# Routed experts of the last feed-forward: token rows sorted by expert on the chip, in place of every expert over every token

## The reference, cut to what matters

```
def _L1_ffn_ref(x, w12, w3, router_w, expert_bias, sw1, sw2, sw3):
    shared_out = jax.nn.silu(x @ sw1.T) * (x @ sw2.T) @ sw3.T
    scores = jax.nn.sigmoid(x @ router_w.T)
    _, top_idx = jax.lax.top_k(scores + expert_bias, 2)
    top_scores = jnp.take_along_axis(scores, top_idx, axis=-1)
    top_scores = top_scores / (top_scores.sum(-1, keepdims=True) + 1e-09)
    ...
    h12 = jnp.einsum('td,ehd->teh', flat_x, w12)
    h1, h2 = jnp.split(h12, 2, axis=-1)
    out_e = jnp.einsum('teh,edh->ted', jax.nn.silu(h1) * h2, w3)
    routed_out = jnp.einsum('ted,te->td', out_e, combine)
    return shared_out + routed_out
x = _layernorm(x + _L1_ffn_ref(x, ...))
```

## Time and profile before

| | us |
|---|---|
| median of 3 runs (lowest, highest) | 1739.21 (1738.74, 1739.77) |
| profiled execution, its own time | 1737.75 |
| its span | 1735.9 |
| last feed-forward, from its first product to its last, each sequence | 144 |

### The profile page before, as it was taken

How to read it: one execution, slowest core, us unless ns; L and a number is a source line. 1 busy time by engine, 2 the same in 40 slices (tenths; PEclk the granted TensorE clock), 3 DMA queues, 4 the chain that set the end, 5 groups by cost and what they waited for, 6 DMA issues and landing times.

```text
span 1735.9 us, 33253 instructions
## 1 busy us (share of the span) xinstructions
PE 1629.3 (94%) x10924; PEld 1401.3 (81%) x10924; DVE 1140.3 (66%) x2654; ACT 936.1 (54%) x1942; POOL 581.2 (33%) x518
## 2 busy tenths in 40 slices
PE   4999999999898999899989999999989989998998
PEld 3888989889787677588878889898988867767887
DVE  7666767676535778455776676766756467765567
ACT  3666565555444577543356655556554437773443
POOL 2554444454460102111126355444555320030120
PEclk9999999999899899999999999999999989999999
DMA  4100000000110423101010000000002123311110
GB/s 132 37 25 16 25 1 15 24 16 1 46 57 15 74 44 67 51 28 46 10 51 23 19 16 25 15 24 0 16 1 64 39 53 56 50 48 43 37 46 25
DMA packets 35213, 60.16 MB, mean 35 GB/s; under 512 B 7989, under 2 KB 22069, under 8 KB 33769
## 3 DMA queue, kind: packets, MB, share of 16 engines
q1 hardware_dynamic: 35064, 58.28, 12.7%
HBM read 42.24 MB, written 3.42 MB: 26 GB/s over the span
## 4 chain that ended last, share of the span: by engine, by line
PE 68%; DVE 11%; ACT 8%; issue 7%; POOL 2%; SPq 1%; DMA 1%; ACTq 0%; DVEq 0%; POOLq 0%
PE ps L346 17%; PE ps L348 16%; PE ps L347 16%; PE ps L901 5%; PE ps L931 4%; PE ps L954 4%; ACT E L1141 3%; DVE nmax L1452 3%; PE ps L762 2%; POOL E L1777 1%; ACT PT_h L1123 1%; DVE On L1394 1%; PE ps L916 1%; PE ps L938 1%; PE ps L701 1%
## 5 line engine op out<-in xcount | busy, mean ns | idle before, releaser
L1141 ACT ACTIVATE E<-ps,nmax 128x128 f32<-128x128 f32 (+7 forms) x256 | 188.8, 741 | 206.9 <-DVE nmax L1452 206.2
L1774 POOL TENSOR_SCALAR E<-E,mixc 128x128 f32<-128x128 f32 (+7 forms) x128 | 97.3, 761 | 381.7 <-DVE mixc L1422 381.7
L1248 ACT ACTIVATE PT<-ps 128x512 f32<-128x512 f32 x288 | 157.9, 599 | 63.4 <-PE ps L938 30.0
L1452 DVE TENSOR_REDUCE nmax<-ps 128x1 f32<-128x128 f32 (+7 forms) x256 | 182.9, 749 | 12.9 <-PE ps L739 12.8
L1777 POOL TENSOR_TENSOR E<-E 128x128 f32<-128x128 f32 (+7 forms) x128 | 182.4, 1425 | 10.7
L1760 POOL TENSOR_TENSOR Fw_l<-Fw_raw,Fw_h 128x768 fp32r<-128x768 f32 x48 | 88.8, 1850 | 262.6 <-ACT Fw_h L1188 261.8
L346 PE MATMUL ps<-V_h,PT_h 128*128 128x256 f32 x576 | 167.5, 291 | 0.0
L346 PE MATMUL ps<-XT_h,Fw_h 128*128 128x512 f32 x384 | 156.4, 407 | 9.0 <-DVE XT_l L1325 9.0
L347 PE MATMUL ps<-V_l,PT_h 128*128 128x256 f32 x576 | 163.1, 283 | 0.0
L348 PE MATMUL ps<-V_h,PT_l 128*128 128x256 f32 x576 | 163.0, 283 | 0.0
L1495 DVE TENSOR_TENSOR Hf<-ps,silu_g 128x512 f32<-128x512 f32 x96 | 66.4, 691 | 140.1 <-PE ps L348 138.0
(11 more groups left out here) (211 smaller groups left out, 4641.4 us busy)
## 6 DMA issues: line engine op xcount, KB each, us to landing
Fw_raw<-in_fa SPq DMA_DIRECT2D x48, 256.0 KB, 2.6
Wa_raw<-in_wa SPq DMA_DIRECT2D x9, 1024.0 KB, 4.9
Wo_raw<-in_wo SPq DMA_DIRECT2D x8, 512.0 KB, 3.9
Fw_raw<-in_fb SPq DMA_DIRECT2D x32, 128.0 KB, 2.6
KS<-QK_h SPq DMA_DIRECT2D x56, 64.0 KB
QS<-QK_h SPq DMA_DIRECT2D x56, 64.0 KB
Xn<-in_x SPq DMA_DIRECT2D x3, 1024.0 KB, 5.8
Fw_raw<-w2s SPq DMA_DIRECT2D x16, 128.0 KB, 2.6
```

Of the source, the lines that this page charges most:

```text
L1141: nc.scalar.activation(e[:, 0:w], ps[m][:, 0:w], ACT.Exp, bias=nmax[:, s % 4, m:m + 1], accum_out=lsum[:, s % 4, m:m + 1]).then_inc(exp_do ...
L1248: nc.scalar.activation(PT[:, at:at + HALF], bank1(RING1 + n % RING1), ACT.Exp, scale=SCALE1).then_inc(t_used, 1)
L1452: nc.vector.tensor_reduce(nmax[:, s % 4, m:m + 1], ps[m][:, 0:(s % NT + 1) * P], AX.X, ALU.max, negate=True).then_inc(nmax_ready[m], 1)
L1774: nc.gpsimd.tensor_scalar(e2, e2, mixc[:, n % 4:n % 4 + 1], 1.0, ALU.mult, ALU.mult).then_inc(mix_scaled, 1)
```

## The change

The 16 expert steps are gone. In their place:

- **Ranks.** The router's portions stand at shared steps 3 to 6, and go on: a product of the picks with a triangle of ones and nine small products on PE (`rank_tokens`) count each token's place among its expert's tokens. DVE adds each expert's first tile and writes the row number as an integer (`place_i`), two per token, and the expert of each of 23 tiles (`expert`). 35 DVE instructions instead of 20.
- **Scatter.** POOL issues 16 indirect DMAs, each sending 128 rows of X (1 KB a row) to their places in `xs` in DRAM, after two of its last three weight splits; the third stands behind the fourth scatter. `xs` is filled first with input rows by three DRAM-to-DRAM DMAs of 2.9 MB at the program's start.
- **Load.** SP waits for all 16 and loads `xs` back in six DMAs (xg), and PE waits for the first two (1 MB).
- **23 tiles.** Between shared steps 27 and 28 PE runs `routed`: each tile of 128 rows is turned (2), multiplied with its expert's gate and up (6 products of 256 columns), turned once after the silu, and multiplied down (3 of 256 columns), one stage of each of four tiles in a round. PE reads the expert's number into a register each round. ACT has four short instructions a round and DVE three. SP stores each result to `ys`.
- **Gather.** POOL waits for all stores of `ys` and issues 16 indirect DMAs that fetch each token's two rows (yg). Meanwhile PE does shared steps 28 to 31. DVE then adds the rows with their shares (`add_experts`, 16 instructions), and statistics and layer norm of both halves follow.
- All experts' weights (3 MB) are loaded at once at the stage's start and split by ACT at shared steps 0 to 3 and by POOL behind that. The load of Xn stands behind the last store of `ys`.

```diff
 QUAD = 4
 FW_RING, H_RING = 5, 3
 STEPS = 2 * CHUNKS
-S_SHARED, S_ROUTED = 2 * CH_F0, 2 * (CH_F0 + CH_SHARED)
+S_SHARED = 2 * CH_F0
+S_MOE = STEPS - QUAD
+TILES = (TOP * T + EXPERTS * (P - 1)) // P
...
+        rows = d["xs"].shape[0]
+        sp.dma_start(d["xs"][0:T], d["x"][0]).then_inc(xs_init, 16)
+        sp.dma_start(d["xs"][T:2 * T], d["x"][1]).then_inc(xs_init, 16)
+        sp.dma_start(d["xs"][2 * T:rows], d["x"][1][0:rows - 2 * T]).then_inc(xs_init, 16)
...
-            load_x(B - 1)
+            sp.dma_start(moe[:], d["moe"].partition_broadcast(P)).then_inc(moe_in, 16)
+            sp.dma_start(tri[:], d["tri"]).then_inc(moe_in, 16)
+            for i in range(ER_LOADS):
+                e = tile(i, 2)
+                sp.dma_start(E_raw[:, e], d["fe"][e].rearrange("e p n -> p e n")).then_inc(er_in[i], 16)
             for c in range(EARLY[-1] + 1, CHUNKS):
                 load_chunk(b, c, d["fb"][c - CH_F0])
+            sp.wait_ge(er_lo, EXPERTS * b + EXPERTS)
+            sp.nop(nofuse=True)
+            sp.wait_ge(sc_out, 16 * TOP * NT * (b + 1))
+            for i in range(LOADS_X):
+                k = slice(i * QUAD, min(TILES, (i + 1) * QUAD))
+                sp.dma_start(xg[:, k], d["xs"].rearrange("(k p) n -> p k n", p=P)[:, k]).then_inc(xg_in[i // 2], 16)
+            for k in range(TILES):
+                sp.wait_ge(ry_copy, TILES * b + k + 1)
+                sp.dma_start(d["ys"][tile(k)], yr[k % 3][:]).then_inc(yr_out[k % 3], 16)
+            load_x(B - 1)
             for q in range(STORES):
                 sp.wait_ge(ln_done, LN_B * b + LN_B - NT + (q + 1) * (NT // STORES))
...
+                if s == S_MOE:
+                    routed(b)
...
+        def routed(b):
+            N = TILES * b
+
+            def turn_tokens(k):
+
+                pe.wait_ge(xg_in[k // (2 * QUAD)], 32 * b + 32)
+                if k >= 2:
+                    pe.wait_ge(rx_lo, N + k - 1)
+                else:
+                    pe.wait_ge(gu_used, STEPS * b + S_MOE + 1)
+                for c in range(KC):
+                    mm = nc.tensor.transpose(xt_bank[k % 2][:, tile(c)], xg[:, k, tile(c)], ident[:])
...
+            def gate_up_tile(k, e):
+
+                pe.wait_ge(rx_lo, N + k + 1)
+                if k >= 2:
+                    pe.wait_ge(rm_done, N + k - 1)
+                else:
+                    pe.wait_ge(gu_used, STEPS * b + S_MOE + 2)
+                for c in range(KC):
+                    w = tile(c, 2 * P)
+                    mm = pass3(pe, xt_bank[2 + k % 2][:, 0:2 * P], xr_h[k % 2][:, c], xr_l[k % 2][:, c],
+                               E_h[:, bass.ds(e, 1), w], E_l[:, bass.ds(e, 1), w], c == 0, c == KC - 1)
...
+            pe.wait_ge(er_lo, EXPERTS * b + EXPERTS)
+            pe.wait_ge(rt_dve, R_B * b + R_PLACE)
+            owner = {}
+            for i in range(TILES + 3):
+                if i < TILES:
+                    turn_tokens(i)
+                if i < 2:
+                    down(b, S_MOE - 2 + i)
+                if 1 <= i <= TILES:
+                    owner[i - 1] = pe.value_load(expert[0:1, i - 1:i], min_val=0, max_val=EXPERTS - 1)
+                    gate_up_tile(i - 1, owner[i - 1])
+                if 2 <= i <= TILES + 1:
+                    turn_gated(i - 2)
+                if i >= 3:
+                    down_tile(i - 3, owner[i - 3])
...
+                k = i - 3
+                if 0 <= k < TILES:
+                    act.wait_ge(rd_mm, N + k + 1)
+                    uses = len(range(k % 3, TILES, 3))
+                    if k >= 3:
+                        act.wait_ge(yr_out[k % 3], 16 * (uses * b + k // 3))
+                    nc.scalar.copy(yr[k % 3][:], ring[1][:, 0:HID]).then_inc(ry_copy, 1)
...
+        def take(b, h):
+
+
+            dve.wait_ge(down_mm, STEPS * b + STEPS - QUAD * (2 - h) + QUAD + H_RING)
+            if h == 0:
+                dve.wait_ge(sc_out, 16 * TOP * NT * (b + 1))
+            for t in range(4 * h, 4 * h + 4):
+                ins = residual(b, 3, t, out_tile(t))
             ins.then_inc(y_taken, 1)
...
+        def add_experts(b, h):
+
+            dve.wait_ge(yg_in[h], 16 * TOP * (NT // 2) * (b + 1))
+            dve.wait_ge(y_taken, 2 * b + h + 1)
+            dve.nop(nofuse=True)
+            for c in range(TOP):
+                for t in range(4 * h, 4 * h + 4):
+                    if c:
+                        dve.wait_ge(y_first, NT * b + t + 1)
+                    ins = nc.vector.scalar_tensor_tensor(out=X[:, t, :], in0=yg[:, c * NT + t, :], scalar=share[:, c, t:t + 1],
+                                                         in1=X[:, t, :], op0=ALU.mult, op1=ALU.add)
+                    ins.then_inc(z_done if c else y_first, 1)
+            for t in range(4 * h, 4 * h + 4):
+                stats(b, 3, t)
+            moments(b, 3, h)
...
+            elif part == 5:
+                counts = rank[:, NT].unsqueeze(2).to_broadcast([P, EXPERTS, EXPERTS])
+                then(nc.vector.tensor_tensor(more[:], counts, steps, ALU.is_gt))
+                then(nc.vector.tensor_reduce(tiles_e[:], more[:], AX.X, ALU.add))
+                then(nc.vector.tensor_tensor(more[:], tiles_e[:].unsqueeze(1).to_broadcast([P, EXPERTS, EXPERTS]), before, ALU.mult))
+                then(nc.vector.tensor_reduce(base_e[:], more[:], AX.X, ALU.add))
+                then(nc.vector.scalar_tensor_tensor(out=rank[:, 0:NT], in0=over_t(base_e), scalar=float(P), in1=rank[:, 0:NT],
+                                                    op0=ALU.mult, op1=ALU.add))
+            elif part == 6:
+                then(nc.vector.tensor_tensor(over[:], picks[:], over_picks(rank[:, 0:NT]), ALU.mult))
+                then(nc.vector.tensor_reduce(place[:], over[:], AX.X, ALU.add))
+                then(nc.vector.tensor_copy(place_i[:], place[:]))
+                then(nc.vector.tensor_tensor(tiles_e[0:1], tiles_e[0:1], base_e[0:1], ALU.add))
+                ends = tiles_e[0:1].unsqueeze(1).to_broadcast([1, TILES, EXPERTS])
+                then(nc.vector.tensor_tensor(past[:], ends, moe[0:1, EXPERTS * (EXPERTS + 1):].unsqueeze(2).to_broadcast(
+                    [1, TILES, EXPERTS]), ALU.is_le))
+                then(nc.vector.tensor_reduce(expert_f[:], past[:], AX.X, ALU.add))
             else:
+                then(nc.vector.tensor_scalar(expert[:], expert_f[:], float(EXPERTS - 1), None, ALU.min))
...
+                pool.wait_ge(er_hi, EXPERTS * b + e + 1)
+                low(E_l[:, e], E_raw[:, e], E_h[:, e]).then_inc(er_lo, 1)
+            for c in range(EARLY[-1] + 1, CHUNKS - 1):
                 ffn_split(b, c)
+            pool.wait_ge(xs_init, 48)
+            pool.wait_ge(rt_dve, R_B * b + R_PLACE)
+            pool.nop(nofuse=True)
+            for t in range(NT):
+                for c in range(TOP):
+                    nc.gpsimd.indirect_dma_start(d["xs"], bass.IndirectOffsetOnAxis(place_i[:, c, t:t + 1], 0), X[:, t, :],
+                                                 None).then_inc(sc_out, 16)
+                if t == 1:
+                    ffn_split(b, CHUNKS - 1)
+            for i in range(3):
+                pool.wait_ge(yr_out[i], 16 * len(range(i, TILES, 3)) * (b + 1))
+            pool.nop(nofuse=True)
+            for h in range(2):
+                for t in range(4 * h, 4 * h + 4):
+                    for c in range(TOP):
+                        nc.gpsimd.indirect_dma_start(yg[:, c * NT + t, :], None, d["ys"],
+                                                     bass.IndirectOffsetOnAxis(place_i[:, c, t:t + 1], 0)).then_inc(yg_in[h], 16)
 
 
```

More of the change, by code:

```diff
@@ L25 @@
 BF16 = mybir.dt.bfloat16
+I32 = mybir.dt.int32
+U32 = mybir.dt.uint32
 ACT = mybir.ActivationFunctionType
@@ L171, in program @@
     s = ctx
+    with ExitStack() as r:
+        E_raw = sb("E_raw", [P, EXPERTS, FFN_COLS], F32, r)
+        sc = sb("sc", [P, NT, EXPERTS], F32, r)
+        sel = sb("sel", [P, NT, EXPERTS], F32, r)
+        ta = sb("ta", [P, NT, EXPERTS], F32, r)
+        comb = sb("comb", [P, NT, EXPERTS], F32, r)[:]
+        tm = sb("tm", [P, NT], F32, r)
+        moe = sb("moe", [P, EXPERTS * (EXPERTS + 1) + TILES], F32, r)
+        tri = sb("tri", [P, 2, P], F32, r)
+        picks = sb("picks", [P, TOP, NT, EXPERTS], F32, r)
+        both = sb("both", [P, NT, EXPERTS], F32, r)
+        over = sb("over", [P, TOP, NT, EXPERTS], F32, r)
+        rank = sb("rank", [P, NT + 1, EXPERTS], F32, r)
+        more = sb("more", [P, EXPERTS, EXPERTS], F32, r)
+        tiles_e = sb("tiles_e", [P, EXPERTS], F32, r)
+        base_e = sb("base_e", [P, EXPERTS], F32, r)
+        place = sb("place", [P, TOP, NT], F32, r)
+        place_i = sb("place_i", [P, TOP, NT], U32, r)
+        share = sb("share", [P, TOP, NT], F32, r)
+        past = sb("past", [1, TILES, EXPERTS], F32, r)
+        expert_f = sb("expert_f", [1, TILES], F32, r)
+        expert = sb("expert", [1, TILES], I32, r)
+    with ExitStack() as r:
```

(59 more changed lines are left out.)

196 lines of the change are left out of this document (141 added, 55 removed).

## The result

The changed kernel takes 1768.6 us (median of 4 runs, 1764.5 to 1771.0), the kernel before, run beside it, 1739.0 (1738.7 to 1739.8). The ratio is 1.017, with a 95% interval of 1.0155 to 1.0187: slower by 29.6 us, where 1769 was predicted. The profiled execution took 1764.45 us, the lowest of the four, with a span of 1762.6.

The account below looks back on a forecast made before the run. PE, busy 94% of the span, was taken to bound the kernel. The terms summed to +15.4 us a sequence, +30.8 for two, on 1737.75: 1768.5, stated as 1769 us, with 1705 to 1832 for 8 times in 10.

Parts of the forecast that it names:

- the hand-over in the round: In each tile round, PE waits once on ACT's or DVE's results: 0.56 us, making a round 2.0 us.
- the gathers on the way out: After the last tile, 16 gathers on POOL, 21.6 us, were to hold DVE idle about 10 us, ended by yg's DMA.
- Steps removed: In the last feed-forward, 16 expert steps of 4.23 us each leave PE's path: -67.7 us a sequence.
- Ranks and router: PE's nine small products, about 1.2 us, and its waits for DVE's 35 router instructions: +4.0 us, bounds +1.5 and +6.
- Stall: Ahead of the first tile, PE stands still for scatters, landing and row load: 31.0 less 14.2, +16.8 us.
- c: Time for each indirect DMA on POOL, scatter or gather: taken as 1.35 us, the middle of 0.84 and 1.85.
- Tiles: 23 tile rounds of 2.0 us on PE, plus DVE's first additions and the first tile's way through: +50.5, bounds 37.6 and 64.3.
- the load's price: PE's register load in each round, floor about 0.6 us; in place of the 0.56, about 2 us more in all.
- Clock: PE's products after the longer pause ahead of the tiles and the loop's end run at the lower clock: +1.5 us.
- Gather and way out: From the last tile's product through gathers and DVE's layer norm, 35.2 us against 24.9: +10.3 us a sequence.
- the cheap case: Rival: indirect DMAs at 0.84 us and tile rounds of 1.7 us make the kernel faster, 1717 us; chance 0.31.
- The case in which DVE holds up POOL's address work: Rival: DVE's H_l subtractions in four steps each stop a POOL scatter, 2.8 us a sequence, about 1774; chance 0.05.

## Why the prediction was right

The time was right to 0.4 us, and that closely by luck: the four runs alone spread over 6.5 us, the sum of +30.8 stands against +29.6 between the medians and +26.7 between the two traces, and two large terms came out in size with a wrong cause: the hand-over in the round and the gathers on the way out. Point by point, for the first sequence:

1. *Steps removed, -67.7.* Right; a step in the changed kernel lasts 4.23 us too.
2. *Ranks and router, +4.0.* PE waits 1.8 us for DVE and its rank products take 2.2: 4.0, though split otherwise (2.8 and 1.2 were taken). DVE's router instructions of 1.30 and 1.52 us beside POOL's splits are there. What was missed is the clock: PE runs at 0.71 of full speed for the 5.8 us from then, which costs some 1.6. By step 24 the stage is 5.8 us late in all (775.7 against 770.0, with a start 0.1 earlier).
3. *Stall, +16.8.* 16.3 measured, with c = 1.27 in place of 1.35. One for one with the number of scatters. Two small errors offset each other: from the first scatter to the first turn it is 29.2 us and not 31.0, and PE has 12.9 us of work from there and not 14.2.
4. *Tiles, +50.5.* From the first turn to the last tile's product, 809.15 to 863.1, less the 2.9 of two downs that were due anyway: 51.1. The round is 1.97 us, 2.0 was said. But the step of the prediction that put 0.56 a round on a hand-over to ACT and DVE failed: in a steady round no hand-over costs PE anything, its own work is 1.40 and the other 0.57 is the register load. Hand-overs cost PE only at the two ends, 2.5 us at the first tile and 1.2 at the last. The prediction had the load's price as an alternative to the hand-over, in a sentence of its own, and took the wrong one of two with the same number; that this did not show in the time is luck.
5. *Clock, +1.5.* After the stall the clock is at 0.51, near the lower level of 1.2 GHz, for 3.3 us, some 1.5 us lost, which stand in the 51.1 of point 4. The 1.6 behind the wait for the ranks were not foreseen. A third loss is on the way out: the kernel before is at 1.00 there, the changed one at 0.51 over 886.0 to 891.0, behind a wait of 4.0 us, and again behind its wait of 7.6 us for K_l. PE and ACT at the next Q, after and before:

```profile
901.56 0.79 PE L405 MATMUL ps<-XT_h,Wa_h 128*128 128x512 f32 x1 [7.57 <-DVE K_l L1567]
904.53 0.69 ACT L1248 ACTIVATE Q_h<-ps,ba 128x512 fp32r<-128x512 f32 x1 [2.42 <-PE ps L407]
```

```profile
887.91 0.50 PE L346 MATMUL ps<-XT_h,Wa_h 128*128 128x512 f32 x1
889.59 0.69 ACT L1096 ACTIVATE Q_h<-ps,ba 128x512 fp32r<-128x512 f32 x1 [0.79 <-PE ps L348]
```

From the first product of Q to ACT's Q_h it is 2.97 us in place of 1.68, so 1.3 lost, and this stands in point 6. In all the clock takes 4.4 us of the first sequence: the term was a third of what it should have been.

6. *Gather and way out, +10.3.* From PE's last product to DVE's first Q_l it is 905.25 - 881.69 = 23.6 us, before it was 890.32 - 877.48 = 12.8: +10.7. Right in size, wrong in cause: I let the gathers end it and predicted DVE idle for 10 us, ended by a DMA of yg. There is no such wait. 9.4 of it is DVE's list: its last additions of PSUM, then 16 additions and both halves' statistics, where most of the kernel before's list is done by PE's last product. What ends it is the second half's mv, at 895.7, for which ACT's square root waits with K_h behind it; DVE's last 3 us of layer norm are beside this path. The other 1.3 is the clock of point 5. Halving the gathers changed nothing. So the step that put the gathers last failed: with their rows there at 889.5 and wanted at 890.7, they are just short of it.

These add up to 5.8 + 16.3 + 51.1 - 67.7 + 10.7 = +16.2. PE's last steps win back about 1.2, 0.9 of it two waits for DVE's X that the changed kernel does not have. That leaves +15.0, as between the two traces (905.25 - 890.32, with a start 0.1 earlier). The second sequence has +13.6 to the end of DVE's layer norm, where no product at the lower clock follows, and +14.3 to the end of the span. Between them, in the next sequence's attention, the changed trace is 2.5 us shorter than the one before (687.7 against 690.2 from Q_l to the next stage), in part in a stretch in which the clock of the kernel before is at 0.96 and its own at 1.00. No edit reaches there, and over the twelve traces this part lasts 686.8 to 693.6 us, so the 2.5 lies within what single executions differ by; what causes it stays open.

Of the rivals, the cheap case had c = 0.84, and the busy time of an indirect DMA is near that (0.96), but POOL issues the next only 0.30 later. The case in which DVE holds up POOL's address work is there in small, as the last section tells. One sum of the prediction does not come out: c from 1.1 to 1.6, counted 64 times in terms 3 and 6 of both sequences, moves its time to 1753 and 1785, not to 1742 and 1800.

## What to carry to other kernels

Price every register load on the bounding engine as an instruction of its own, about 0.55 us that six queued products did not hide, and where several values are known together fetch them in one load and at a place where the engine waits. A wait of a few tenths that a trace puts down to another engine's semaphore can be such a load: move the suspected instruction, and see which gap goes. A chain through DRAM (16 indirect DMAs, landing, reload: some 30 us here) pays only as far as other work covers it, so start it at the moment its input is there, and look up which of the deferred instructions is wanted first.

## What the runs showed of the hardware

- A register load on PE: 0.54 to 0.57 us for one register, 6.3 for a load of 23 registers (0.28 each). Behind six queued products a single one costs the same.
- An indirect DMA of 128 rows of 1 KB holds POOL for 0.95 to 0.96 us and the next begins 1.25 to 1.27 after it; the median landing is 2.4 for scatters and 2.8 for gathers. If DVE's subtraction of two SBUF operands is running when it starts, it takes longer, as the second and fourth gather here show (H_l on DVE from 867.56 and 870.38, 0.69 each; the sixth and ninth likewise, 1.25 and 1.42):

```profile
866.41 0.98 POOL L2155 DMA_INDIRECT yg<-ys,place_i  x1 [64.28 <-DMA ys<-yr]
867.70 1.39 POOL L2155 DMA_INDIRECT yg<-ys,place_i  x1 [0.30 <-issue]
869.39 0.95 POOL L2155 DMA_INDIRECT yg<-ys,place_i  x1 [0.30 <-issue]
870.64 1.24 POOL L2155 DMA_INDIRECT yg<-ys,place_i  x1 [0.30 <-issue]
```

The price is 0.3 to 0.47 us and follows what DVE's instruction has left at that moment: 0.55 us left cost 0.44, 0.43 cost 0.29, 0.60 cost 0.47. A scatter that starts just ahead of the same subtraction, and runs beside it, takes its usual time:

```profile
788.53 0.96 POOL L2145 DMA_INDIRECT xs<-X,place_i  x1 [0.30 <-issue]
788.65 0.69 DVE L1692 TENSOR_TENSOR H_l<-Hf,H_h 128x512 fp32r<-128x512 f32 x1 [0.69 <-ACT H_h L1350]
```

The first scatter of the stage does not fit this: it takes 1.20 though H_l starts 0.25 behind it. The Trainium skill (SBUF — State Buffer, SBUF: two separate sides) tells of descriptors that GpSimd cannot write while DVE holds the shared port, 620 ns becoming 3100. The traces agree in kind, but beside instructions of 0.69 us the loss is 0.3 to 0.47 and never near 2.5.
